# Full attention's first scores four banks at a time, longer spreads in the plan, weights split in thirds

## What is computed

```python
x = x + 0.5 * _L0_ffn_ref(_layernorm(x), ...)
x = x + _L0_attn_ref(_layernorm(x), Wq, bq, Wk, bk, Wv, bv, Wo, bo)
x = x + 0.5 * _L0_ffn_ref(_layernorm(x), ...)
```

```python
scores = jnp.einsum('bhqd,bhkd->bhqk', q, k) / np.sqrt(HD)
scores = jnp.where(causal, scores, -jnp.inf)
out = jnp.einsum('bhqk,bhkd->bhqd', softmax(scores), v)
```

## Time and profile before

| | us |
|---|---|
| median of three runs | 1801.35 |
| the three runs | 1801.35, 1790.93, 1801.44 |
| the profiled execution | 1793.28 |
| its span, first to last instruction | 1791.4 |
| granted TensorE clock, mean over the span | 0.948 |

### The profile page before, as it was taken

One profiled execution on the slowest core, in us unless ns is written; L12 is line 12 of the kernel. 1 busy time (PEld: TensorE's weight loads), 2 busy tenths in 40 slices (PEclk: granted clock), 3 DMA queues, 4 the chain that ended last, 5 costly groups with the idle time before them and its releaser, 6 DMA issues.

```text
span 1791.4 us, 48412 instructions
## 1 busy us (share of the span) xinstructions
PE 1562.1 (87%) x17754; PEld 1259.1 (70%) x17754; DVE 1448.5 (81%) x2953; ACT 1311.4 (73%) x3846; POOL 1303.5 (73%) x1562
## 2 busy tenths in 40 slices
PE   3789799898988899887989899998889988898987
PEld 3667677666767777766767777776667777677776
DVE  6778789777877889877887998886788897687895
ACT  2588687667677888686779886766578877587885
POOL 7899857368648988687699997732489785469891
PEclk9799999889989999998999998997899999799999
DMA  5001101202010111111010111020210101100000
GB/s 154 16 20 28 42 23 49 92 11 60 13 49 19 25 30 49 33 25 51 24 27 19 25 27 49 21 91 26 71 26 19 52 19 55 51 22 22 19 23 13
DMA packets 49346, 66.75 MB, mean 37 GB/s; under 512 B 8114, under 2 KB 32220, under 8 KB 49116
## 3 DMA queue, kind: packets, MB, share of 16 engines
q1 hardware_dynamic: 49116, 63.66, 12.6%
HBM read 22.75 MB, written 15.73 MB: 21 GB/s over the span
## 4 chain that ended last, share of the span: by engine, by line
POOL 30%; DVE 22%; PE 21%; ACT 11%; DMA 7%; issue 7%; SPq 2%; POOLq 0%; ACTq 0%; DVEq 0%
POOL sums L1198 10%; POOL parts L1188 8%; POOL parts L1202 7%; ACT probs L1264 6%; DVE parts L1568 6%; DMA laid_dram<-halves 4%; PE bank L1640 4%; PE bank L1827 3%; DVE neg_full L1447 3%; DMA stacked_k<-laid_dram 3%; PE bank L1690 2%; PE bank L1788 2%; DVE sums L1575 2%; PE bank L1872 2%; POOL sums L1195 2%
## 5 line engine op out<-in xcount | busy, mean ns | idle before, releaser
L1188 POOL TENSOR_TENSOR parts<-parts 128x256 f32<-128x256 f32 x512 | 382.6, 772 | 136.2 <-DVE parts L1568 134.8
L1198 POOL TENSOR_TENSOR sums<-sums,neg_half 128x8 f32<-128x8 f32 x256 | 434.3, 1696 | 21.3
L1264 ACT ACTIVATE probs<-bank,neg_max 128x128 f32<-128x128 f32 x1024 | 366.2, 406 | 56.4 <-DVE neg_max L1447 54.5
L1568 DVE TENSOR_TENSOR parts<-bank,rope 128x1024 f32<-128x1024 f32 x256 | 309.0, 1216 | 48.3 <-ACT squares L1322 46.7
L1202 POOL TENSOR_TENSOR parts<-parts,sums 128x512 f32<-128x512 f32 x256 | 280.1, 1094 | 37.3 <-POOL sums L1198 0.9
L1264 ACT ACTIVATION_READ_ACCUMULATOR probs<-bank,neg_max 128x1 f32 x1024 | 249.9, 246 | 0.0
L1872 PE MATMUL bank<-ident,parts 128*128 128x128 f32 x1024 | 163.9, 284 | 67.2 <-POOL parts L1202 64.5
L1322 ACT ACTIVATE squares<-bank 128x512 f32<-128x512 f32 x256 | 158.8, 624 | 64.3 <-PE bank L1640 39.2
L1872 PEld LDWEIGHTS bank<-ident,parts 128*128 128x128 f32 x1024 | 117.4, 144 | 99.8 <-issue 71.8
L1640 PE MATMUL bank<-wqkv_hi,h_hi 128*128 128x512 f32 x384 | 179.3, 467 | 4.0 <-ACT q_t L1340 0.8
L1447 DVE TENSOR_REDUCE neg_max<-bank 128x4 f32<-128x512 f32 x256 | 164.2, 681 | 20.6 <-PE bank L1711 19.9
(11 more groups left out here) (146 smaller groups left out, 3902.6 us busy)
## 6 DMA issues: line engine op xcount, KB each, us to landing
between<-val SPq DMA_DIRECT2D x192, 128.0 KB, 2.3
laid_dram<-halves SPq DMA_DIRECT2D x96, 128.0 KB
stacked_q<-laid_dram SPq DMA_DIRECT2D x16, 512.0 KB, 3.2
stacked_k<-laid_dram SPq DMA_DIRECT2D x16, 512.0 KB, 4.3
x_sb<-in_L_attn_x_dram SPq DMA_DIRECT2D x16, 128.0 KB, 2.5
out_dram<-x_sb SPq DMA_DIRECT2D x16, 128.0 KB, 1.8
raw_qkv<-in_L_ffn_wqkv_dram SPq DMA_DIRECT2D x2, 768.0 KB, 4.7
laid_dram<-plain SPq DMA_DIRECT2D x8, 128.0 KB
```

The costliest lines, as they stand in the source:

```text
L1188: last = nc.gpsimd.tensor_tensor(joined[:, :, dst], joined[:, :, dst], sines[:, :, src], ALU.add)
L1198: nc.gpsimd.tensor_tensor(sums[:, u], sums[:, u], neg_half[:], ALU.pow).then_inc(sems["pool_step"], 1)
L1264: last = nc.scalar.activation(probs[:, u, block:block + wide].rearrange("p b j -> p (b j)"), bank[:, at:at + P * wide], ACT.Exp, bias=neg_ ...
L1568: nc.vector.tensor_tensor(parts[:, u].rearrange("p o (h d) -> p o h d", d=LOCAL_D), bank[:].rearrange("p (o h d) -> p o h d", o=1, d=LOCAL ...
```

## The change

Six things change. The plan's constants that are only numbers (all of START_AT, DUE, PHASE_DUE, LATER, PASSES; a new table NUDGE that shifts the due dates of single steps) are left out of the diff below; STRETCH goes from 2.2324 to 2.402.

1. A full-attention `S` step covers all sixteen heads: four banks, on the four groups of 32 partitions; three steps a sequence instead of six. `E` stays with two banks.
2. SCORES_AHEAD goes from 3 to 5.
3. SPREADING goes from 9.5 to 14.5 us and WRITING from 3.6 to 7.5 us. q's three writes are issued before k's, and each of the two has its own semaphore, so that q is read back once q is written.
4. QKV weights of layer 0 are loaded in three DMAs, q's first and before the table, and are split in six `READY` steps instead of two (layer 1 too, though its load stays whole).
5. The clearing of buffers goes from POOL to DVE.
6. The masks become two steps, one for local and one for full attention.

```diff
@@ -46,7 +46,7 @@
-SCORES_AHEAD = 3
+SCORES_AHEAD = 5
...
-PIECES = [("qkv_hi", 0), ("qkv_lo", 0), ("table", 0), ("w1_scaled", 0), ("w1_hi", 0), ("w1_lo", 0), ("qkv_hi", 1),
-          ("qkv_lo", 1), ("table", 1), ("w1_scaled", 1), ("w1_hi", 1), ("w1_lo", 1), ("wf_scaled", 0), ("wf_hi", 0),
-          ("wf_lo", 0)]
+QKV = ("q", "k", "v")
+PIECES = [(f"{x}_{half}", 0) for x in QKV for half in ("hi", "lo")] + [("table", 0)] + [
+    (f"w1_{x}", 0) for x in ("scaled", "hi", "lo")] + [(f"{x}_{half}", 1) for x in QKV for half in ("hi", "lo")] + [
+    ("table", 1)] + [(f"w1_{x}", 1) for x in ("scaled", "hi", "lo")] + [(f"wf_{x}", 0) for x in ("scaled", "hi", "lo")]
...
-WRITING = 3.6
-SPREADING = 9.5
+WRITING = 7.5
+SPREADING = 14.5
...
-        return [(POOL, 5.4)]
+        return [(POOL, 3.8 if n else 5.4)]
     if kind in ("S", "E"):
-        return [(PE, (0.7 if n % 3 else 0.85) if is_full(ph) else 1.15)]
+        return [(PE, 1.23 if not is_full(ph) else (0.88 if n else 1.25) if kind == "S" else (0.7 if n % 3 else 0.97))]
...
+    if is_full(ph) and kind == "S":
+        return [("X", s, ph, 3 * u + n) for u in range(UNIT)]
     if is_full(ph):
-        return [("X" if kind == "S" else "Y", s, ph, 6 * (n // 3) + n % 3 + k) for k in (0, 3)]
+        return [("Y", s, ph, 6 * (n // 3) + n % 3 + k) for k in (0, 3)]
...
-    return ("S" if kind == "X" else "E", s, ph, k // 6 * 3 + k % 3 if is_full(ph) else k // 2)
+    if kind == "X":
+        return ("S", s, ph, k % 3 if is_full(ph) else k // 2)
+    return ("E", s, ph, k // 6 * 3 + k % 3)
...
-        WRITES = 16 * 2 * len(PARTS)
+        WRITES = 16 * len(PARTS)
...
+            def load_qkv(m):
+                sp.dma_start(raw_qkv[:, 0, INNER * m:INNER * (m + 1)],
+                             a["L0_ffn_wqkv"][0, :, INNER * m:INNER * (m + 1)]).then_inc(entry_loaded[m], 16)
+
             load_x(0)
+            load_qkv(0)
+            load_x(1)
...
-                sp.dma_start(rope[:, 1], a["rope"].rearrange("(t p) a b d -> p t a b d", p=P)).then_inc(entry_loaded, 16)
-                sp.dma_start(raw_qkv[:, 0], a["L0_ffn_wqkv"][0]).then_inc(entry_loaded, 16)
+                sp.dma_start(rope[:, 1], a["rope"].rearrange("(t p) a b d -> p t a b d", p=P)).then_inc(scales_loaded, 16)
...
-                for s in range(1, STREAMS):
+                load_qkv(1)
+                load_qkv(2)
+                for s in range(2, STREAMS):
                     load_x(s)
...
-                for part, of in enumerate(PARTS):
-                    for w in range(2):
-                        sp.dma_start(laid[u, w, :, part], halves[SET_OF[step[1:3]]][:, of[w]].bitcast(F32)).then_inc(written[u], 16)
+                for w in range(2):
+                    for part, of in enumerate(PARTS):
+                        sp.dma_start(laid[u, w, :, part], halves[SET_OF[step[1:3]]][:, of[w]].bitcast(F32)).then_inc(written[u][w], 16)
...
-                sp.wait_ge(written[u], WRITES * nth)
                 sp.wait_ge(spread_pads, 16 * 2 * SPREADS)
                 for w, dst in enumerate((stacked_q, stacked_k)):
+                    sp.wait_ge(written[u][w], WRITES * nth)
...
-            for k in range(SETS):
-                nc.gpsimd.memset(between[k][0:HALF, 0], 0.0)
-            nc.gpsimd.memset(val_full[:], 0.0)
-            nc.gpsimd.memset(spaced[:], 0.0)
-            nc.gpsimd.memset(pads[:], 0.0).then_inc(cleared, 1)
-            n += 1
-            pool.wait_ge(cleared, n)
-            for j in range(P // PAD_D):
-                nc.gpsimd.memset(pads[PAD_D * j:PAD_D * j + 2 * CHUNKS, 1], 1.0).then_inc(cleared, 1)
-                n += 1
-                pool.wait_ge(cleared, n)
-            for k in range(VALUES_FULL):
-                for t in range(TILES):
-                    ones = val_full[:, k, t, 0:FULL_HEADS * VAL_D].rearrange("p (h d) -> p h d", d=VAL_D)[:, :, FULL_D:VAL_D]
-                    last = nc.gpsimd.memset(ones, 1.0)
-            last.then_inc(pads_cleared, 1)
...
+            def make_masks_full():
+                nonlocal n
+                nc.gpsimd.memset(mask_full[:], 0.0)
+                nc.gpsimd.memset(mask_turned[:], 0.0).then_inc(cleared, 1)
+                n += 1
+                pool.wait_ge(cleared, n)
+                for rows in (slice(0, HALF), slice(HALF, P)):
+                    for half in range(2):
+                        select(mask_full[rows, half:half + 1], HALF * half, -1, 1, ALU.is_ge, MASKED)
+                        select(mask_turned[rows, half:half + 1], -HALF * half, 1, -1, ALU.is_ge, MASKED)
+                nc.gpsimd.memset(pool_mark[:], 0.0).then_inc(sems["masked"], 1)
+
...
+            nc.vector.memset(pads[:], 0.0).then_inc(zeroed, 1)
+            nc.vector.memset(val_full[:], 0.0).then_inc(zeroed, 1)
             for s in range(STREAMS):
 
                 nc.vector.memset(state[s][HALF:C, 0:1], 0.0)
+            for k in range(SETS):
+                nc.vector.memset(between[k][0:HALF, 0], 0.0)
+            nc.vector.memset(spaced[:], 0.0)
+            dve.wait_ge(zeroed, 2)
+            for j in range(P // PAD_D):
+                nc.vector.memset(pads[PAD_D * j:PAD_D * j + 2 * CHUNKS, 1], 1.0)
+            for k in range(VALUES_FULL):
+                for t in range(TILES):
+                    ones = val_full[:, k, t, 0:FULL_HEADS * VAL_D].rearrange("p (h d) -> p h d", d=VAL_D)[:, :, FULL_D:VAL_D]
+                    last = nc.vector.memset(ones, 1.0)
+            last.then_inc(pads_cleared, 1)
             for step, part in DVE_ORDER:
...
-                if what == "qkv_hi":
+                if what[0] in QKV:
+                    x = QKV.index(what[0])
+                    cols = slice(INNER * x, INNER * (x + 1))
+                if what in ("q_hi", "k_hi", "v_hi"):
                     if m == 0:
-                        dve.wait_ge(entry_loaded, 32)
+                        dve.wait_ge(entry_loaded[x], 16)
                     else:
                         dve.wait_ge(w_loaded, 16 * N_WLOADS)
-                    last = nc.vector.tensor_copy(wqkv_hi[:, m], raw_qkv[:, m])
-                if what == "qkv_lo":
-                    last = nc.vector.tensor_tensor(wqkv_lo[:, m], raw_qkv[:, m], wqkv_hi[:, m].bitcast(F32), ALU.subtract)
+                    last = nc.vector.tensor_copy(wqkv_hi[:, m, cols], raw_qkv[:, m, cols])
+                if what in ("q_lo", "k_lo", "v_lo"):
+                    last = nc.vector.tensor_tensor(wqkv_lo[:, m, cols], raw_qkv[:, m, cols], wqkv_hi[:, m, cols].bitcast(F32),
+                                                   ALU.subtract)
                 if what == "table":
...
-                if step == FIRST_SCORED:
-                    pe.wait_ge(sems["masked"], 1)
+                if step in FIRST_MASKED:
+                    pe.wait_ge(sems["masked"], NTH["masked"]["MASKS", 0, 0, int(is_full(ph))])
...
-                    pair, of = n // 3, n % 3
+                    first, of = 2 * (n // 3), n % 3
...
-                                rows = slice(HALF * odd, HALF * (odd + 1))
+                                rows = slice(HALF * (odd % 2), HALF * (odd % 2 + 1))
...
-                            rows = slice(PAD_D * (2 * pair + odd), PAD_D * (2 * pair + odd + 1))
+                            rows = slice(PAD_D * (first + odd), PAD_D * (first + odd + 1))
```

More of the change, by code:

```diff
@@ new lines, with come @@
+STORING = 6.5
+PIECE_LASTS = {"table": 0.95, "w1_scaled": 0.6, "w1_hi": 0.6, "w1_lo": 0.85, "wf_scaled": 0.4, "wf_hi": 0.5, "wf_lo": 0.7}
+PIECE_COMES = {("q_hi", 0): 6.0, ("k_hi", 0): 9.0, ("v_hi", 0): 9.5, ("table", 0): 9.0, ("q_hi", 1): 20.0, ("k_hi", 1): 20.0,
+               ("v_hi", 1): 20.0, ("wf_scaled", 0): 31.0}
+X_COMES = (5.0, 6.0, 9.5, 10.0, 10.5, 11.0, 11.5, 12.0)
+def come(step, part):
+    kind, s, ph, n = step
+    if part == 0 and kind == "LNX" and ph == 0 and s < STREAMS:
+        return X_COMES[s]
+    if kind == "READY":
+        return PIECE_COMES.get(PIECES[n], 0.0)
+    if kind == "FOLD":
+        return 31.0 if n == LAYERS else 25.0 if part else 15.0
+    return 0.0
@@ L213, in passes @@
     if kind == "READY":
-        return [(DVE, PIECE_LASTS[PIECES[n][0]])]
+        what = PIECES[n][0]
+        return [(DVE, PIECE_LASTS.get(what, 0.47 if what.endswith("hi") else 0.63))]
     if kind == "FOLD":
@@ L318, in weights_of @@
         l = QKV_LAYER[PHASES[ph][1]]
-        return made(("qkv_hi", l), ("qkv_lo", l))
+        x = "v" if kind == "VAL" else QKV[n % 2]
+        return made((f"{x}_hi", l), (f"{x}_lo", l))
     if kind == "Q" and part == PRODUCT:
@@ L332, in weights_of @@
         what, m = PIECES[n]
-        before = {"qkv_lo": "qkv_hi", "w1_hi": "w1_scaled", "w1_lo": "w1_hi", "wf_hi": "wf_scaled", "wf_lo": "wf_hi"}
-        if what in before:
-            return made((before[what], m))
+        name, half = what.split("_") if "_" in what else (what, "")
+        if half == "lo":
+            return made((name + "_hi", m))
+        if half == "hi" and name not in QKV:
```

(25 more changed lines are left out.)

68 lines of the change are left out of this document (35 added, 33 removed), and 93 rows, old and new, of tables (DUE, LATER, NUDGE).

## The result

The changed kernel takes 1714.27 us (median of four runs, 1712.97 to 1721.53), the kernel before 1801.11 in the same comparison: a ratio of 0.954 with an interval of 0.950 to 0.958. Repeated on another chip the ratio was 0.951 (0.949 to 0.953). The forecast was 1730 and 71 us of gain; 87 were measured. The profiled execution took 1712.97 us, with a span of 1711.1 and a mean clock of 0.96.

The account below looks back on a forecast made before the run. TensorE was taken to bound the kernel, losing time to DMA waits and half clock. Terms -8 - 12 - 47 = -67 us from 1793.3 gave 1726, plus half of an 8 us run offset: 1730 us, range 1692 to 1785.

Parts of the forecast that it names:

- The bound: Whole kernel: TensorE sets the time, busy 1562.1 of 1791.4 us; its waits for late data are paid as idle and half clock.
- The start: Kernel start: clears to VectorE, masks later, weights in thirds bring TensorE's first instruction to 10.4 us; -8 us (0 to -10).
- First scores: Full-attention score steps: four banks a step overlap more and save shape changes; 12 us gained, bounds 0 and 25.
- Spread: First scores waiting for stacked_k's DMA: larger SPREADING and WRITING move them later; 47 us gained, 60% of 78.
- (a): Rival at the first scores: the array overlaps nothing, all else as forecast; 1742 us, chance 0.16.
- (b): Rival: DMA waits go but return as other waits and half clock; only start and scores remain, 1777 us, chance 0.28.
- (c): Rival: first-score steps wait for four free banks, 2.73 us in each of 48 steps; slower, 1861 us, chance 0.08.
- They only reorder; I count 0: Five ahead, new due dates, new durations, layer 2's weights in thirds: same instructions in another order, counted as 0 us.

Follow-up runs that it names:

- b_early: Kernel before, same orders, but stacked_q and stacked_k filled early from a DRAM area of zeros and pads (output not the reference's): 1733.09 us, ratio 0.966.
- a_all_undone: Changed kernel, same orders except masks first on GpSimd; bank pairs kept apart, k's data 4 to 5 us later, clears on GpSimd: 1749.28 us, ratio 0.970.
- a_apart: Changed kernel, same orders; in each first-score step all work of two banks, masks included, precedes that of the other two: 1726.66 us, repeated 1729.83.
- a_slow_again: Changed kernel, same orders, two small DMA round trips before k's read so its data come 4 to 5 us later; repeat run: 1727.66 us, ratio 0.961.
- a_pairs: Changed kernel, same orders and banks; products in a first-score step issued through banks 0 and 1, then 2 and 3: 1712.94 us, ratio 0.953.

## Why the prediction was right, and where it was off

**The bound, right.** TensorE in its fixed order, held by waits for late data: b_early took those waits away and gained 62 to 65 us.

**The start, right in the sum and off in its way.** 8 us forecast, 7 measured. TensorE begins at 11.27 and not at 10.4: the statistics ended at 8.85 instead of 8.63, and from GpSimd's first var_eps (8.93) to TensorE it took 2.34 us instead of 1.8, with a first rstd of 1.14 us where it had been 0.71. The first QKV product comes at 19.75, 2.2 us earlier and not 8, since GpSimd makes the masks for full attention between the first and the second norm (10.42 to 15.34), and VectorE's split of the first state (17.99) stands in its list behind the second norm. The start after:

```profile
7.44 0.27 DVE L1551 BATCH_NORM_STATS2 bn<-x_sb 128x6 f32<-128x128 f32 x1
...
8.93 0.30 POOL L1214 TENSOR_SCALAR var_eps<-mean_var 128x2 f32<-128x2 f32 x1 [2.98 <-DVE mean_var L1556]
...
11.27 0.66 PE L1901 MATMUL bank<-ident,normal 128*128 128x128 f32 x2 [11.27 <-DVE normal L1563]
17.13 0.69 PE L1901 MATMUL bank<-ident,normal 128*128 128x128 f32 x2 [5.21 <-DVE normal L1563]
...
19.75 0.77 PE L1702 MATMUL bank<-wqkv_hi,h_hi 128*128 128x512 f32 x1
```

That 6.6 us of time came out nevertheless, I can only report. The clears on VectorE were not hidden, as the prediction said they would be. It took 7.86 us for the time at which VectorE has data, but that is when the tile landed which stood first in VectorE's list; stream 0's x was there at 2.90. In the changed kernel x tiles landed at 2.82 and 4.41, the clears (6.0 us, not 5.2) held VectorE until 7.44, and GpSimd stood for 2.98 us until the statistics were done. With them ahead of the clears the start could come up to 3 us sooner, an estimate from that wait; no run tried it.

**First scores, wrong in the reading.** The term was 12 us with a highest bound of 25; 23 to 25 us of TensorE and 17 us of time were measured. The term took a saving of TensorE for a saving of time, which hides part of the error. The failed step is "107 ns is one product after the other: two row groups show no overlap". 107 ns was a mean over two groups that were both at work: in the step at 331.46 of the earlier trace rows the first two products start 3 ns apart, and the next two 0.22 us later. A group takes 0.215 us for one of its 256-column products, two groups give one each 107 ns, four give one each 54. The same holds for 128 columns: eight products in two groups and sixteen in four both took 0.60 us (the step at 374.07 above goes on with its products from 374.63 to 375.23). Nor were the weight loads the next limit at 65 ns each: sixteen of them took 0.53 us in the changed kernel, where eight took 0.52. The Trainium skill's rule that a load costs by its columns (TensorE: Matmul & The Clock Gate, section on LDWEIGHTS) is right for one load: at full clock loads of 32x128 took 181 to 187 ns and one of 128x128 took 186. The Trainium skill also says (same page, Part 3) that a load overlaps with matmuls in flight only if its row group is another. The trace has more than that: loads for different row groups ran beside each other. I used half of the page. The loads of four groups in the changed kernel:

```profile
220.61 0.53 PEld L1752 LDWEIGHTS bank<-stacked_k,stacked_q 32*128 32x128 f32 x16 [0.41 <-issue]
```

**Spread, right in kind, too small in the old order, not separable in the new.** The full price of the ten waits was put at 78 us and 60% of it taken, 47. b_early makes the price 62 to 65, about 80%: the discount of 40%, for work that would be missed later, was too large there, and the backlog of the earlier trace rows was the better witness. In the changed kernel the term can't be measured alone. Its 87 us less 17 and 7 for the other two parts leave 63, and a_all_undone gives 55 and 15, that is 70, for the order as a whole: later first scores, but also four banks in the plan, other dates and NUDGE, which the prediction put at nothing. That 63 to 70 is so near to b_early's 62 to 65 fits the account and does not prove it. What is shown of the new order is that ten waits became one and that 49 us less ran at half clock, 137 us instead of 186 (118 in b_early, so the new order has some new places of its own).

How the 80 us between the two profiled executions are made up can be read from the two pages and a_apart, and it is not how the terms were: 7 are the start, 25 are other idle time (229 to 197 in all), 23 to 25 are work that the packing saved, and some 25 are the same work at the higher clock.

**Rivals.** (a), no overlap, fell by a_apart and by the starts of single products. (b), waits come back elsewhere, fell by b_early and by the list of waits after. (c), four banks at once are too many, fell too: the full-attention score steps after waited for VectorE's neg_full 2.0 us in five waits, the longest 0.7 us, where they had waited 2.4 us in seven.

**"They only reorder; I count 0".** The sum came out near because the new dates fit the new numbers. That was luck in the method: the same two numbers with the old dates cost 95 us (1899 against 1805 on that chip). The rival that should have stood there is a plan whose tables do not fit, and its size, some 95 us and more, exceeds all the terms together. That 1730 lies within 16 us of 1714 is owed to an order that happened to fit.

**Still open.** The 63 to 70 us of the order cannot be split among later first scores, four banks in the plan, two more score banks ahead and better durations: each changes the whole order, and alone, with dates made for the others, none can be priced.

## What to carry to other kernels

If engines run fixed orders, a duration in the plan that is too short for a DMA is paid at every place where the data are late, and often in the clock as well (1.5 times the wait in b_early, 1.2 times in a_slow_again): look for waits on DMAs behind which the engine then runs without a hole. To price such a part, keep the order and change the thing itself, by data that are there early or two hops later; a new plan with one changed number measures the plan's tables and not the number. And before calling parallel units serial, divide the time by the products of one unit, not by those of all.

## What the runs showed of the hardware

Products of 32 rows in different row groups ran side by side, whatever order they were issued in: 0.44 us for four 256-column products in two groups, for eight in four groups issued around, and for eight issued pair by pair (a_pairs). Masks between them, in another shape of the array, ended that: 1.33 us instead of 0.79 for the step (what a change of shape costs by itself, no run separates). Mask products in 64x64 tiles gained less by the doubling: four of 256 columns took 0.23 us from start to the next step (618.64 to 618.87), eight took 0.35 (608.32 to 608.67).
